# Batch 0's last gathers land beside each other and VectorE sums them, in a fused attention, expert and attention kernel

## Chip, cores and metric

The kernel runs on one core of a Trainium2 chip. The metric is the device time of one execution in microseconds (us), median of several runs. Every engine has its own instruction queue, taken in order: TensorE (PE), VectorE (DVE), ScalarE (ACT), GpSimd (POOL), and SyncE (SP), which issues plain DMAs. Gathers with a list of row numbers (indirect DMAs) are issued by GpSimd, and so are DMAs that add what they fetch onto their destination.

## The reference, cut to what matters

There are 8 batches of 256 tokens of 512 numbers: 2048 tokens. The second step, and the beginning of the third, are what this case is about.

```python
x = x + tanh(g_xattn[0]) * causal_attention(layernorm(x), ctx, ctx)
x = x + tanh(g_ffn[0])   * experts(layernorm(x))     # 32 experts, each token goes to 8 of them
x = x + tanh(g_xattn[1]) * cross_attention(layernorm(x), ctx, ...)
x = x + tanh(g_ffn[1])   * ternary_linear(layernorm(x))
# experts: every (token, choice) has a slot in an expert's table; y = silu(xg @ w_gate) * (xg @ w_up) @ w_down
#          out[token] += weight * y[slot]            for each of the token's 8 choices
# cross_attention: q = rms_norm(x @ w_q.T + b_q, g_q), k = rms_norm(ctx @ w_k.T + b_k, g_k), v = ctx @ w_v.T + b_v
#          softmax(q k.T / sqrt(32)) v for 16 heads, then @ w_o.T + b_o
```

## The kernel before

There are three stages, one block of instructions for each. A block ends in a barrier: no engine begins the next one before all have issued what they have in this one.

**layer0** is the first attention and sends each token's row to 8 slots of a table in DRAM. **experts** runs 160 tiles of 128 slots through the experts' weights. For a tile PE turns the rows (L1293), multiplies by gate and up (L1305), turns the hidden rows (L1316) and multiplies by down (L1329); ACT scales the result into `ysb` (L1379), and SP stores that to `y_tiles` in DRAM (L1162), counted on four semaphores `y_out`. GpSimd loads the raw weights of each expert to `raw` (two buffers), which DVE splits into halves `wh` and `wl`. **layer1** is the second attention and the ternary layer, a loop over the 8 batches with 16 attention steps each.

*The gathers.* A token's 8 results are fetched from `y_tiles` and added to its row of `xs` (the running x, all 2048 tokens in SBUF) at the beginning of layer1 and during it. One gather fetches 128 rows of 2 KB: one of the two token tiles `t` of a batch, one of 8 choices. "A turn" is the two gathers of one choice; each batch has 8 turns, 16 gathers. A gather that adds to the same rows as an earlier one waits until that has landed. The choices are sorted, so turn 0 of batch 0 needs only that all but the last 7 tiles are stored, turn 7 needs all of them (`add_first`).

In batch 0, even turns add into `xs` (semaphores `y_added`) and odd ones into a second buffer `odd` (`odd_added`); its first gather there is plain (L431), all others add (L430). Turns 0 to 3 are issued in the experts block, turns 4 to 7 in layer1's. Later batches have all 8 turns added into `xs` by `add_rows` (L430). Batch 1's 16 gathers follow at once, with small jobs of GpSimd between them: 4 gathers stand before its job "P1" and 4 before "P3", 8 behind. In every attention step `s` of batch `b` GpSimd does its jobs of the step, waits for step s's probabilities, and issues one gather for batch `b + 2`.

*The beginning of layer1.* Before batch 0's attention all engines run the lists `BEGIN1`. For one batch the work in pieces is:
- "sc", "T0", "T1": the context rows are split to fp16 halves by ACT (L1588) and DVE (L1653) and turned (PE L1548, ACT L1593). "P0", "P1": their product for K, 12 matmuls of 128x512 each (PE L1542), read out by DVE (L1659). PE needs the read of one product before it begins the next.
- "xc": layernorm's statistics of x by DVE (L1636, L1640, L1642, semaphore `x_var`), which need every gather of the batch; GpSimd makes the inverse root (L1615). "xn": DVE normalizes (L1646). "sx", "T2", "T3": the split and turn of that (ACT L1583, DVE L1653). "P2", "P3": the products for Q in batch 0, "P4", "P5" for V; in later batches P2 is V's and "P3", "P4" Q's.
- After a pair of products ACT squares and sums them (L1599), and GpSimd makes the factors of rms norm in three small operations (L1622, L1624, L1626). Its job "P1" is that for K; "P3" in batch 0 and "P4" in the others is that for Q. DVE's "r" (L1666) waits for the latter; "k0" to "k3" (L349, L355, L361) and "S0" to "S7" (L372, L379) make the heads' stacks from the results.

In the loop the pieces of the next batch are dealt out to steps by the table `PREP1`. For GpSimd it says "xc" at step 5, "P1" at step 7, "P4" at step 11; for DVE "xc" and "xn" at step 4 and "r" at step 10. An attention step on DVE begins with the row maxima for two steps ahead (L325), then ACT's exponentials (L293), PE's turn of the probabilities (L278) and the product with V (L258).

Of the kernel before, what the change touches and what calls it, by code (L numbers as in the profile page):

```python
# [18 lines left out]
P = 128  # L19
# [17 lines left out]
SENT = 6  # L37
LAST_ADDS = 4
BY_ACT = (1, 5)
# [70 lines left out]
def over_batches(first, body, last):  # L110
# [80 lines left out]
class Attention:  # L191
# [5 lines left out]

    def __init__(self, nc, sb, sem, bank, tag, causal, scale, v, id32, id16, idb, maskb):
# [9 lines left out]
        self.probs = sb(tag + "probs", [P, 2, 2, S])  # L208
        self.probsT = sb(tag + "probsT", [P, 2, 4 * P])
        self.sums = sb(tag + "sums", [P, 2, QT, NH])  # L210
        self.outT = sb(tag + "outT", [P, 2, QT, H])
# [171 lines left out]
class Shared:  # L383


    def __init__(self, nc, es):
# [26 lines left out]
        self.bank = [es.enter_context(nc.psum_tensor(f"bank{i}", [P, 512], F32)) for i in range(8)]  # L413
        room = sb("room", [P, 11 * H])
        self.vec = room[:, 0 : 7 * H].rearrange("p (k h) -> p k h", h=H)
        self.cbuf1 = room[:, 7 * H : 9 * H].rearrange("p (t h) -> p t h", h=H)
        self.odd = room[:, 9 * H : 11 * H].rearrange("p (t h) -> p t h", h=H)
        self.xe = room[:, 0 : 2 * QT * ROW].rearrange("p (a t r) -> p a t r", a=2, t=QT)
# [4 lines left out]
        self.y_out = [es.enter_context(nc.semaphore(f"y_out{i}")) for i in range(NY)]  # L423
        self.odd_added = [es.enter_context(nc.semaphore(f"odd_added{t}")) for t in range(QT)]

    def gather(self, nc, to, n, t, k, add):
# [6 lines left out]
    def add_first(self, nc, pool, turn, t):  # L433

        k, n = TOPK - 1 - turn, turn // 2
        if t == 0:
            for i in range(NY):
                pool.wait_ge(self.y_out[i], 16 * len(range(i, MT - k, NY)))
        if turn % 2:
            if n > 0:  # L440
                pool.wait_ge(self.odd_added[t], 16 * n)
            self.gather(nc, self.odd[:, t, :], 0, t, k, n > 0).then_inc(self.odd_added[t], 16)
        else:
            if n > 0:
                pool.wait_ge(self.y_added[t], 16 * n)
            self.gather(nc, self.xs[:, t, :], 0, t, k, True).then_inc(self.y_added[t], 16)

    def add_rows(self, nc, pool, n, i):

        turn, t = divmod(i, QT)  # L450
        done = TOPK * n + turn - TOPK // 2
        pool.wait_ge(self.y_added[t], 16 * done)
# [3 lines left out]
class Plan:  # L456


    def __init__(self, nc, es):
        def sb(name, shape, dt=F32):  # L460
# [21 lines left out]
        self.t_dve = sb("t_dve", [1, MT], I32)  # L482
        self.raw = sb("raw", [P, NR, WEXP])
        self.absum = sb("absum", [P, HC])
# [626 lines left out]
def experts(nc, shared, plan, proj, w_experts, mats, ternary, ctx, vecs):  # L1111

    es = ExitStack()
    with es:
# [81 lines left out]
        def _(pool):  # L1196
# [69 lines left out]
            for e in range(NR + 1, E):  # L1266
# [15 lines left out]
        def _(pe):  # L1282
# [120 lines left out]
        def _(dve):  # L1403
# [36 lines left out]
            for t in range(3):  # L1440
                e = dve.value_load(t_e[0:1, t : t + 1])
                if t == 0:
# [5 lines left out]
            def step(t):  # L1448
                code = dve.value_load(t_dve[0:1, t.column()])
                with dve.If((code & 1) > 0):  # L1450
# [8 lines left out]
def layer1(nc, shared, weights, ctx, out):  # L1459

    es = ExitStack()
    with es:
# [9 lines left out]
        vbuf = sb("vbuf", [P, 2, QT, H])  # L1472
        at = Attention(nc, sb, sem, bank, "l1_", False, D**-0.5 / (SC_Q * SC_K), vbuf, shared.id32, shared.id16, None, None)

# [19 lines left out]
        rsum = sb("rsum1", [P, QT, NH])  # L1494
        att = sb("att1", [P, QT, H])
        a16 = sb("a16", [P, QT, 2, H], F16)
# [3 lines left out]

        g_made, sc_made, both = sem("g_made"), sem("sc_made"), sem("both")
        y_added, ctx_in = shared.y_added, shared.ctx_in
# [127 lines left out]
        def dve_prep_(dve, b, piece, chain):  # L1630
            v = nc.vector
            k = int(piece[1]) if piece[1:].isdigit() else 0
            if piece == "xc":
                for t in range(QT):
                    dve.wait_ge(y_added[t], 16 * (TOPK * (b.n + 1) - TOPK // 2))
                    chain.mark(v.bn_stats(st6[:, 0, t, :], mine(b, t)))  # L1636
# [156 lines left out]
        def _(pool):  # L1793
# [13 lines left out]

            before = {"P1": 4, "xc": 0, "P3": 4}
            for piece in BEGIN1["pool"]:
# [4 lines left out]
            def body(b, prep, post):  # L1814
                for s in range(STEPS):
# [34 lines left out]
        def _(dve):  # L1850
# [65 lines left out]
def flamingo(nc, x, ctx, g_xattn, g_ffn, gate_w, w_experts, mats, vecs, ternary, out):  # L1916
    with ExitStack() as es:
        shared = Shared(nc, es)
        weights = Projections(nc, es)
        with ExitStack() as es_plan:  # L1920
            plan = Plan(nc, es_plan)
            layer0(nc, shared, plan, weights, x, ctx, g_xattn, g_ffn, gate_w, w_experts, mats, ternary)
# [39 lines left out]
```

## Time and profile before

| what | value |
|---|---|
| median of 3 runs | 1558.16 us (1550.44 to 1563.45) |
| span of the profiled execution, first to last instruction | 1525.3 us |
| median less the span | 32.9 us |
| busy share: PE, DVE, ACT, POOL | 86%, 64%, 60%, 34% |
| mean granted TensorE clock, share of 2.4 GHz | 0.939 |

The page gives no time of its own for the profiled execution, only its span; the runs' times hold some 33 us more, which lie ahead of and behind the instructions. Times of rows are us from the start of the span. In a timeline row stand the start, how long, engine, line, operation, what it writes and reads, and in brackets how long the engine was idle before it and what ended that. A row of a merged group has the time of all its instructions.

### The profile page before, as it was taken

How to read it: one execution, taken by the hardware profiler on the slowest of the kernel's cores; microseconds unless marked ns; L12 is line 12 of the kernel's file. 1: busy time of each engine (PE TensorE's matmuls, PEld its weight loads, DVE VectorE, ACT ScalarE, POOL GpSimd, SP SyncE). 2: the span in 40 equal slices, each digit the busy share in tenths (PEclk: the TensorE clock that was granted, in tenths of full speed). 3: DMA queues.
4: the chain of work that ended last, by engine and by line, in shares of the span. 5: the costliest groups of instructions: out<-in, count | busy, mean ns of one | idle time of the engine just before them, and what ended most of it. 6: DMA issues, size and time to landing. Idle time of an engine off the chain costs nothing.

```text
span 1525.3 us, 37150 instructions
## 1 busy us (share of the span) xinstructions
PE 1309.4 (86%) x10733; PEld 834.6 (55%) x10734; DVE 972.8 (64%) x2387; ACT 920.1 (60%) x2261; POOL 520.1 (34%) x531
## 2 busy tenths in 40 slices
PE   5888888837999999999999999477989889898984
PEld 3656655524556666665666666144556555555552
DVE  5888888755456665655655633255787777776853
ACT  4777777724556666666666666244766667667661
POOL 1044444455333433332000001665554444541000
PEclk9988888968999999999999999688999999999997
DMA  2044344458888767767676545775654555642000
GB/s 72 29 173 180 146 146 151 156 213 304 269 285 282 256 219 261 238 217 244 218 242 222 181 149 154 126 111 83 98 99 65 104 82 84 100 65 52 15 1 28
DMA packets 96131, 233.39 MB, mean 153 GB/s; under 512 B 11808, under 2 KB 11808, under 8 KB 91424
## 3 DMA queue, kind: packets, MB, share of 16 engines
q0 software_dynamic: 33712, 113.79, 29.8%
q1 hardware_dynamic: 62320, 118.34, 23.3%
q8 instruction: 55, 0.90, 0.3%
q14 instruction: 44, 0.36, 0.1%
HBM read 140.84 MB, written 91.24 MB: 152 GB/s over the span
## 4 chain that ended last, share of the span: by engine, by line
PE 45%; DMA 9%; DVE 9%; issue 8%; ACT 3%; POOL 3%; SPq 1%; DVEq 0%; ACTq 0%; POOLq 0%
PE bank L1305 18%; PE bank L1329 10%; PE bank L1542 6%; DMA xs<-y_tiles,slot_ix 5%; PE bank L1293 4%; PE bank L258 2%; PE bank L1316 1%; PE bank L278 1%; DMA xg<-x_slots 1%; DVE l_nmax L325 1%; PE bank L1548 1%; POOL xs L430 1%; DMA x_slots<-blank 1%; DVE l_stack L379 1%; PE bank L240 1%
## 5 line engine op out<-in xcount | busy, mean ns | idle before, releaser
L1305 PE MATMUL bank<-wh,xT 128*128 x1280 | 343.3, 330 | 4.7 <-DVE hp L1420 4.4
L430 POOL DMA_INDIRECT xs<-y_tiles,slot_ix x120 | 194.6, 1622 | 234.2 <-DMA y_tiles<-ysb 99.1
L293 ACT ACTIVATE l_probs<-bank,l_bias 128x256 f32<-128x256 f32 (+1 forms) x512 | 224.4, 449 | 64.4 <-DVE l_bias L327 64.0
L1305 PE MATMUL bank<-wl,xT 128*128 x640 | 211.4, 330 | 0.0
L325 DVE TENSOR_REDUCE l_nmax<-bank 128x2 f32<-128x512 f32 (+1 forms) x256 | 158.1, 617 | 70.8 <-PE bank L240 41.3
L1410 DVE SCALAR_TENSOR_TENSOR hv<-bank,sg 128x192 f32<-128x192 f32 x160 | 56.9, 356 | 227.5 <-ACT sg L1364 203.5
L1379 ACT ACTIVATE ysb<-bank,xg 128x512 f32<-128x512 f32 x160 | 109.9, 687 | 119.1 <-PE bank L1329 119.1
L305 ACT ACTIVATE l_probsT<-bank 128x512 f32<-128x512 f32 (+1 forms) x256 | 140.0, 547 | 65.6 <-PE bank L278 65.2
L1358 ACT ACTIVATE xT<-bank 128x1024 f16<-128x1024 f16 x160 | 162.5, 1016 | 15.0 <-PE bank L1293 14.8
L1305 PEld LDWEIGHTS bank<-wh,xT 128*128 128x128 f16 x1280 | 126.5, 99 | 81.3 <-issue 11.1
L1329 PE MATMUL bank<-wh,hT 128*128 x480 | 156.1, 380 | 0.9 <-issue 0.9
L240 PE MATMUL bank<-l_stack 128*128 128x256 f16 (+1 forms) x512 | 105.7, 275 | 59.1 <-ACT l_probs L293 49.3
L278 PE MATMUL bank<-id,l_probs 128*128 128x128 f32 x896 | 149.7, 286 | 2.1 <-ACT l_probsT L305 0.5
L699 POOL DMA_INDIRECT x_slots<-room,slot_ix x112 | 113.4, 1013 | 108.3 <-issue 47.0
L1542 PE MATMUL bank<-w_hi,halfT 128*128 128x512 f16 x384 | 125.9, 390 | 18.9 <-DVE accb L1659 17.1
L1200 POOL DMA_DIRECT2D raw<-in_experts_dram x30 | 16.8, 560 | 334.1 <-DVE wl L1436 333.8
L1364 ACT ACTIVATE sg<-bank 128x192 f32<-128x192 f32 x160 | 52.8, 330 | 113.8 <-PE bank L1305 113.8
L1329 PE MATMUL bank<-wl,hT 128*128 x320 | 121.4, 379 | 0.0
L1293 PEld LDWEIGHTS bank<-id,xg 128*128 128x128 f16 x1280 | 84.9, 99 | 58.7 <-DMA xg<-x_slots 22.6
L1293 PE MATMUL bank<-id,xg 128*128 128x128 f16 x1280 | 98.9, 221 | 19.1 <-DMA xg<-x_slots 18.9
L278 PEld LDWEIGHTS bank<-id,l_probs 128*128 128x128 f32 x896 | 102.6, 147 | 11.7 <-ACT l_probsT L305 7.4
L1436 DVE SCALAR_TENSOR_TENSOR wl<-raw,wh x64 | 95.4, 1491 | 20.0 <-issue 15.9
(246 smaller groups left out, 2538.1 us busy)
## 6 DMA issues: line engine op xcount, KB each, us to landing
xg<-x_slots SPq DMA_DIRECT2D x160, 272.0 KB, 2.8
y_tiles<-ysb SPq DMA_DIRECT2D x160, 256.0 KB, 2.5
raw<-in_experts_dram POOLq DMA_DIRECT2D x30, 1280.0 KB, 7.1
x_slots<-blank SPq DMA_DIRECT2D x33, 272.0 KB, 3.6
xs<-in_x_dram SPq DMA_DIRECT2D x8, 512.0 KB, 4.4
cbuf<-in_ctx_dram SPq DMA_DIRECT2D x8, 512.0 KB, 5.8
stage<-in_mats_dram POOLq DMA_DIRECT2D x4, 1024.0 KB, 7.8
room<-in_ctx_dram SPq DMA_DIRECT2D x8, 512.0 KB, 4.6
```

The source lines that it names most:

```text
L240: last = self.nc.tensor.matmul(o, self.stack[:, b.par, 0, h, qt * P : (qt + 1) * P], self.stack[:, b.par, 1, h, 0:nk], start=True, stop=no ...
L278: last = self.nc.tensor.transpose(self.pT[s % len(self.pT)][:, (2 * kt + u) * P : (2 * kt + u + 1) * P], self.probs[:, s % 2, u, kt * P : ...
L293: last = self.nc.scalar.activation(self.probs[:, s % 2, u, 0:nk], self.pS[s % 2][:, u * S : u * S + nk], ACT.Exp, bias=self.bias[:, s % 4, ...
L305: self.nc.scalar.activation(self.probsT[:, s % 2, 0:w], self.pT[s % len(self.pT)][:, 0:w], ACT.Copy).then_inc(self.probsT_made, 1)
L325: self.nc.vector.tensor_reduce(self.nmax[:, s % 4, :], v, AX, ALU.max).then_inc(self.max_made, 1)
L430: return nc.gpsimd.indirect_dma_start(to, None, self.y_tiles[0 : (MT + 1 - k) * P, :], ix, compute_op=ALU.add)
L699: nc.gpsimd.indirect_dma_start(shared.x_slots, bass.IndirectOffsetOnAxis(ap=slot_ix[:, QT * b.n + t, k % TOPK : k % TOPK + 1], axis=0), xe ...
L1293: last = nc.tensor.transpose(o[:, c * P : (c + 1) * P], rows[:, c * P : (c + 1) * P], id16[:])
L1305: last = nc.tensor.matmul(bGU[t.place % 2][:, 0:GU], xT[:, t.place % 2, xo + c * P : xo + (c + 1) * P], wp[:, bass.ds(w, 1), c * GU : (c + ...
L1329: last = nc.tensor.matmul(bY[t.place % 2][:, :], h, wp[:, bass.ds(w, 1), at : at + H].rearrange("p a w -> p (a w)"), start=k == 0, stop=k ...
L1358: nc.scalar.activation(xT[:, t.place % 2, :], bX[t.place % 2][:, :].bitcast(F16), ACT.Copy).then_inc(x_ready, 1)
L1542: last = nc.tensor.matmul(o, xT[:, xo + c * P : xo + (c + 1) * P], w[:, c * H : (c + 1) * H], start=n == 0, stop=n == len(todo) - 1)
```

## The change

Turns 4 to 7 of batch 0 become plain gathers, each to a place of its own; the places (`landed`, five of them, the first is the former `odd`) lie in the memory of the raw expert weights, which therefore becomes `late`, shared by all stages. Plain gathers wait for no other gather, only for the stores and, once, for the last weights' split. Turns 4 and 5 are now issued at the end of the experts block, turns 6 and 7 in layer1. Only turns 0 to 3 still add by DMA. DVE adds the five places to `xs` in pieces "g0" to "g4", ten additions instead of two, spread over the beginning of its list, and its "P0" now stands ahead of "g3", and "P1" ahead of "sx".

GpSimd's order changes: 3 gathers of batch 1 before "xc", 1 before "P1", 4 before "P3", 8 behind. In batch 0's steps it issues no gather at steps 0 to 5, two at each of steps 6 to 11, one at steps 12 to 15. Some buffers of layer1 (probabilities, their turned form, the attention's output, `att1`) move into `late`. Three loads of table values into registers get bounds.

```diff
-LAST_ADDS = 4
+FIRST_TURNS, ADDED_TURNS = 6, 4
...
-    dve=["sc", "xc", "xn", "P0", "sx", "P1", "P2", "k0", "k1", "P3", "S0", "S1", "S2", "S3", "r", "k2", "k3", "S4", "S5", "P4", "S6", "S7", "P5"])
+    dve=["g0", "g1", "sc", "g2", "P0", "g3", "g4", "xc", "xn", "P1", "sx", "P2", "k0", "k1", "P3", "S0", "S1", "S2", "S3", "r", "k2", "k3", "S4", "S5", "P4", "S6", "S7", "P5"])
...
-        if turn % 2:
+        if turn >= ADDED_TURNS:
+            self.gather(nc, self.landed[:, 1 + turn - ADDED_TURNS, t, :], 0, t, k, False).then_inc(self.rows_in[turn - ADDED_TURNS], 16)
+        elif turn % 2:
...
-            for turn in range(TOPK - LAST_ADDS):
+            pool.wait_ge(weights_ready, E)
+            for turn in range(FIRST_TURNS):
...
-                code = pe.value_load(t_pe[0:1, t.column()])
+                code = pe.value_load(t_pe[0:1, t.column()], min_val=0, max_val=E * E)
...
-            for turn in range(TOPK - LAST_ADDS, TOPK):
+            for turn in range(FIRST_TURNS, TOPK):
                 for t in range(QT):
                     shared.add_first(nc, pool, turn, t)
             added = [ROWS]
+            FIRST_ADDS = [0] * 6 + [2] * 6 + [1] * 4
...
-            before = {"P1": 4, "xc": 0, "P3": 4}
+            before = {"xc": 3, "P1": 1, "P3": 4}
...
                     if b.n + 2 < B:
                         pool.wait_ge(at.probs_made, STEPS * b.n + s + 1)
-                        add_next(1)
+                        add_next(1 if b.n else FIRST_ADDS[s])
...
             for piece in BEGIN1["dve"]:
+                if piece[0] == "g":
+                    i = int(piece[1])
+                    for t in range(QT):
+                        if i == 0:
+                            dve.wait_ge(y_added[t], 16 * ADDED_TURNS // 2)
+                            dve.wait_ge(shared.odd_added[t], 16 * ADDED_TURNS // 2)
+                        else:
+                            dve.wait_ge(shared.rows_in[i - 1], 16 * QT)
+                            dve.wait_ge(summed, QT * (i - 1) + t + 1)
+                        v.tensor_tensor(mine(b0, t), mine(b0, t), shared.landed[:, i, t, :], ALU.add).then_inc(summed, 1)
+                    continue
                 if piece == "xc":
-                    for t in range(QT):
-                        dve.wait_ge(y_added[t], 16 * TOPK // 2)
-                        dve.wait_ge(shared.odd_added[t], 16 * TOPK // 2)
-                        v.tensor_tensor(mine(b0, t), mine(b0, t), shared.odd[:, t, :], ALU.add).then_inc(both, 1)
-                    dve.wait_ge(both, QT)
+                    dve.wait_ge(summed, QT * (TOPK - ADDED_TURNS + 1))
```

## Rows read from the trace of the kernel before

**Rows 1.** Busy time by stretch: from:to, length, PE, PEld, DVE, ACT, POOL, clock, DMA share, GB/s.

```profile
400.00:940.00 540.00, 530.95 (x4031) 329.70 (x4030) 301.18 (x806) 332.76 (x576) 116.35 (x144) 0.99 0.69 230
962.00:990.00 28.00, 8.47 (x33) 3.88 (x34) 8.02 (x15) 6.13 (x9) 16.53 (x13) 0.61 0.68 113
```

**Rows 2.** The chain that ended last, 940 to 1100: start, us, what.

```profile
976.50 5.69 DMA room<-y_tiles,slot_ix
...
1019.42 4.98 DMA xs<-y_tiles,slot_ix
1024.40 0.26 issue
...
1043.78 0.77 POOL rstd L1615
```

**Rows 3.** Timeline of VectorE at the beginning of layer1.

```profile
964.32 1.29 DVE L1653 SCALAR_TENSOR_TENSOR l_parts<-room,l_parts 128x512 f16<-128x512 f32 x2 [8.93 <-ACT l_parts L1588]
...
982.29 0.69 DVE L1862 TENSOR_TENSOR xs<-xs,room 128x512 f32<-128x512 f32 x1 [1.28 <-DMA room<-y_tiles,slot_ix]
...
986.48 1.06 DVE L1646 TENSOR_SCALAR accb<-xs,mv,rstd 128x512 f32<-128x512 f32 x2 [0.85 <-POOL rstd L1615]
987.46 0.68 DVE L1659 SCALAR_TENSOR_TENSOR accb<-bank,room 128x512 f32<-128x512 f32 x1
```

**Rows 4.** Timeline of PE: first and second product's beginning, third's.

```profile
967.21 0.61 PE L1542 MATMUL bank<-w_hi,halfT 128*128 128x512 f16 x1 [0.26 <-ACT halfT L1593]
...
988.28 0.58 PE L1542 MATMUL bank<-w_hi,halfT 128*128 128x512 f16 x1 [16.21 <-DVE accb L1659]
...
995.29 0.39 PE L1542 MATMUL bank<-w_hi,halfT 128*128 128x512 f16 x1 [1.55 <-ACT halfT L1593]
```

**Rows 5.** Timeline of VectorE in batch 0's steps.

```profile
1035.57 0.69 DVE L1659 SCALAR_TENSOR_TENSOR accb<-bank,room 128x512 f32<-128x512 f32 x1 [1.01 <-PE bank L1542]
1044.57 1.05 DVE L1646 TENSOR_SCALAR accb<-xs,mv,rstd 128x512 f32<-128x512 f32 x2 [8.31 <-POOL rstd L1615]
...
1065.74 1.40 DVE L1666 SCALAR_TENSOR_TENSOR accb<-accb,rs,room 128x512 f32<-128x512 f32 x2
```

**Rows 6.** Timeline of GpSimd around the end of the experts block.

```profile
949.86 0.98 POOL L431 DMA_INDIRECT room<-y_tiles,slot_ix  x1 [0.30 <-issue]
...
959.80 1.53 POOL L430 DMA_INDIRECT room<-y_tiles,slot_ix  x1 [0.30 <-issue]
962.36 0.10 POOL L1794 MEMSET sc<- 128x2 f32 x1 [1.03 <-POOLq L1114]
...
963.30 1.54 POOL L430 DMA_INDIRECT xs<-y_tiles,slot_ix  x1 [0.80 <-POOL sc L1795]
```

**Rows 7.** DMAs, us to landing: all L430; one plain gather; the store issued at 958.3.

```profile
DMA to landing us min/median/max: 4.6/5.0/7.1
...
room<-y_tiles,slot_ix POOLq DMA_INDIRECT x1, 4.8
...
y_tiles<-ysb SPq DMA_DIRECT2D x1, 256.0 KB, 3.9
```

**Rows 8.** Timeline of ACT: Q's last square; step 6's exponentials.

```profile
1002.98 0.19 ACT L1599 ACTIVATION_READ_ACCUMULATOR junk<-accb 128x1 f32 x1
...
1046.71 0.45 ACT L293 ACTIVATE l_probs<-bank,l_bias 128x256 f32<-128x256 f32 x1
```

**Rows 9.** Timeline of GpSimd: job P3, batch 1's last gather, job P4.

```profile
1006.26 0.19 POOL L1622 TENSOR_SCALAR ss<-ss 128x2 f32<-128x2 f32 x1
...
1027.49 1.54 POOL L430 DMA_INDIRECT xs<-y_tiles,slot_ix  x1 [0.81 <-DMA xs<-y_tiles,slot_ix]
...
1064.26 0.19 POOL L1622 TENSOR_SCALAR ss<-ss 128x2 f32<-128x2 f32 x1 [1.93 <-ACT junk L1599]
```

**Rows 10.** Register instructions: SP's load with bounds; PE's load, one tile.

```profile
L1157 SPq SEQ_ASSERT  x160: 18/18/18, 342.3 to 939.4; - x160
...
L1335 PEldq TENSOR_LOAD <-t_pe x1: 303/303/303, 901.9 to 901.9; - x1
```

More of the change, by code:

```diff
@@ L191, with __init__ @@
 class Attention:
-    def __init__(self, nc, sb, sem, bank, tag, causal, scale, v, id32, id16, idb, maskb):
+    def __init__(self, nc, sb, sem, bank, tag, causal, scale, v, id32, id16, idb, maskb, held=None):
+        held = held or sb
         self.nc, self.causal, self.scale, self.v = nc, causal, scale, v
@@ L207, in __init__ @@
         self.bias = sb(tag + "bias", [P, 4, 2])
-        self.probs = sb(tag + "probs", [P, 2, 2, S])
-        self.probsT = sb(tag + "probsT", [P, 2, 4 * P])
+        self.probs = held(tag + "probs", [P, 2, 2, S])
+        self.probsT = held(tag + "probsT", [P, 2, 4 * P])
         self.sums = sb(tag + "sums", [P, 2, QT, NH])
-        self.outT = sb(tag + "outT", [P, 2, QT, H])
+        self.outT = held(tag + "outT", [P, 2, QT, H])
         self.hi_ready, self.parts_ready = sem(tag + "hi_ready"), sem(tag + "parts_ready")
@@ L413, in __init__ @@
         self.bank = [es.enter_context(nc.psum_tensor(f"bank{i}", [P, 512], F32)) for i in range(8)]
-        room = sb("room", [P, 11 * H])
+        room = sb("room", [P, max(9 * H, 2 * QT * ROW + 3 * QT * H)])
+        self.late = sb("late", [P, NR * WEXP])
         self.vec = room[:, 0 : 7 * H].rearrange("p (k h) -> p k h", h=H)
         self.cbuf1 = room[:, 7 * H : 9 * H].rearrange("p (t h) -> p t h", h=H)
-        self.odd = room[:, 9 * H : 11 * H].rearrange("p (t h) -> p t h", h=H)
+        LANDED = TOPK - ADDED_TURNS + 1
+        self.landed = self.late[:, 0 : LANDED * QT * H].rearrange("p (n t h) -> p n t h", n=LANDED, t=QT)
         self.xe = room[:, 0 : 2 * QT * ROW].rearrange("p (a t r) -> p a t r", a=2, t=QT)
@@ L424, in __init__ @@
         self.odd_added = [es.enter_context(nc.semaphore(f"odd_added{t}")) for t in range(QT)]
+        self.rows_in = [es.enter_context(nc.semaphore(f"rows_in{i}")) for i in range(TOPK - ADDED_TURNS)]
     def gather(self, nc, to, n, t, k, add):
@@ L438, in add_first @@
                 pool.wait_ge(self.y_out[i], 16 * len(range(i, MT - k, NY)))
-        if turn % 2:
+        if turn >= ADDED_TURNS:
+            self.gather(nc, self.landed[:, 1 + turn - ADDED_TURNS, t, :], 0, t, k, False).then_inc(self.rows_in[turn - ADDED_TURNS], 16)
+        elif turn % 2:
             if n > 0:
                 pool.wait_ge(self.odd_added[t], 16 * n)
-            self.gather(nc, self.odd[:, t, :], 0, t, k, n > 0).then_inc(self.odd_added[t], 16)
+            self.gather(nc, self.landed[:, 0, t, :], 0, t, k, n > 0).then_inc(self.odd_added[t], 16)
         else:
@@ L450, in add_rows @@
         turn, t = divmod(i, QT)
-        done = TOPK * n + turn - TOPK // 2
+        done = TOPK * (n - 1) + turn + ADDED_TURNS // 2
         pool.wait_ge(self.y_added[t], 16 * done)
@@ L456, with __init__ @@
 class Plan:
-    def __init__(self, nc, es):
+    def __init__(self, nc, es, shared):
+        self.raw = shared.late[:, :].rearrange("p (r w) -> p r w", r=NR)
         def sb(name, shape, dt=F32):
@@ L1440, in _ @@
             for t in range(3):
-                e = dve.value_load(t_e[0:1, t : t + 1])
+                e = dve.value_load(t_e[0:1, t : t + 1], min_val=0, max_val=E - 1)
                 if t == 0:
@@ L1448, in step @@
             def step(t):
-                code = dve.value_load(t_dve[0:1, t.column()])
+                code = dve.value_load(t_dve[0:1, t.column()], min_val=0, max_val=2**24)
                 with dve.If((code & 1) > 0):
@@ L1472, in layer1, with held @@
         vbuf = sb("vbuf", [P, 2, QT, H])
-        at = Attention(nc, sb, sem, bank, "l1_", False, D**-0.5 / (SC_Q * SC_K), vbuf, shared.id32, shared.id16, None, None)
+        LATER = dict(l1_probs=(0, 2 * 2 * S), l1_probsT=(2 * 2 * S, 2 * 4 * P), l1_outT=(8 * S, 2 * QT * H), att1=(8 * S + 4 * H, QT * H))
+        def held(name, shape, dt=F32):
+            first, n = LATER[name]
+            view = shared.late[:, first : first + n]
+            if dt == F16:
+                view = view.bitcast(F16)
+            letters = "abcd"[: len(shape) - 1]
+            sizes = {k: n for k, n in zip(letters, shape[1:])}
+            return view.rearrange(f"p ({' '.join(letters)}) -> p {' '.join(letters)}", **sizes)
+        at = Attention(nc, sb, sem, bank, "l1_", False, D**-0.5 / (SC_Q * SC_K), vbuf, shared.id32, shared.id16, None, None, held)
         w_hi, w_lo, vec = weights.w_hi, weights.w_lo, shared.vec
@@ L1494, in layer1 @@
         rsum = sb("rsum1", [P, QT, NH])
-        att = sb("att1", [P, QT, H])
+        att = held("att1", [P, QT, H])
         a16 = sb("a16", [P, QT, 2, H], F16)
@@ L1634, in dve_prep_ @@
                 for t in range(QT):
-                    dve.wait_ge(y_added[t], 16 * (TOPK * (b.n + 1) - TOPK // 2))
+                    if b.n > 0:
+                        dve.wait_ge(y_added[t], 16 * (TOPK * b.n + ADDED_TURNS // 2))
                     chain.mark(v.bn_stats(st6[:, 0, t, :], mine(b, t)))
```

5 lines of the change are left out of this document (2 added, 3 removed).

## The prediction

> **What bounds the kernel now.** I read the busy time by stretch first, then the chain of waits, then each engine's timeline where the chain leaves PE. In the experts stage PE is busy 530.95 of 540 us [rows 1]: nothing can be won there, only lost. From 962 to 990, the beginning of layer1, it is busy 8.47 of 28 us, at a mean clock of 0.61. The chain [rows 2] says why: it is on gathers, one behind the other, up to the last one of batch 0, issued at 976.50 and landed 5.69 us later. Then it follows GpSimd up to the inverse root of batch 1 at 1043.78. So the change works in the two places where the chain stands on gathers or on GpSimd's queue:
>
> Stall A, 972 to 988. VectorE is idle until the last gather lands, adds it at 982.29, and begins "xn" at 986.48, so 4.19 us later. The read of the first product stands behind that, at 987.46 [rows 3]; PE therefore waits 16.21 us with the second one [rows 4].
>
> Stall B, 1036 to 1045. VectorE waits 8.31 us for GpSimd's L1615 [rows 5], which stands in GpSimd's queue behind batch 1's gathers and five of batch 2's. Each gather on the same rows waits for the landing of the one two before it.
>
> **The end of the experts block.** GpSimd now issues turns 4 and 5 there. Its last gather before started at 959.80 and took 1.53 us, so it was free at 961.33, and layer1 began at 962.36 [rows 6]: GpSimd was nearly the last engine at the barrier. A plain gather occupies it for 0.98 us, and 0.30 go between two, 1.28 together, against 1.83 for one that adds [rows 6]. Four of them begin at 961.63; the store that turn 5 waits for was issued at 958.3 and landed after 3.9 us [rows 7], in time. GpSimd is free at 961.63 + 4 x 1.28 - 0.30 = 966.45, and layer1 begins at about 967.1 (the distance before was 1.03 us from the end of GpSimd, part of which was SP's last store; I take 0.65, bounds 0.4 and 1.1). Everything of layer1 that isn't waiting for gathers moves 4.7 us later. This is the price of the change.
>
> **Batch 0's landing.** Turns 6 and 7 begin 0.94 us after the block, as turn 4 did [rows 6], at 968.05, and the last of the four at 968.05 + 3 x 1.28, with 0.5 for the last store, about 972.1; it lands after 4.8 [rows 7], at 976.9, where the last landing before was 982.19 [rows 2]. Bounds: landings of 4.6 and of 7.1 [rows 7]. So the rows are there 5.3 us earlier, but VectorE can't use all of it: "P0" now stands before "g3". The first product began at 967.21, 4.85 us after the block, and lasted 4.9 at the half clock (PE was idle for 16.21 us before 988.28, so it ended at 972.07) [rows 4]; "g0" and "g1" ahead of "sc" add about 0.9, since the landing of turn 4 and two additions of 0.69 lie ahead of it. PE is done at 967.1 + 4.85 + 0.9 + 4.9 = 977.75. Then VectorE: 0.69 for the read, four additions of 0.71, 981.3. Before, the second addition ended at 982.98 [rows 3]. From there to "xn" it takes 3.5 us as before, and "xn" begins at 984.8. **Gain at "xn" 1.7 us**, bounds -1 and +4. The three gathers of batch 1 now ahead of GpSimd's inverse root cost nothing: the third waits for the first one's landing, 973.4 + 5.3 = 978.7, and is issued by 980.3, while the root isn't wanted before 984.
>
> **Behind "xn".** The second product is now done before it (its input, the context, was ready; it needs at most 4.9 us after 978.4). Before it held PE from 988.28 on, and T2 and T3 and ACT's copies waited for it, so that the third product began at 995.29 [rows 4]. Now T2 follows "sx" directly; ACT squares P0 and P1 first, and copies T2 at 989.5. The third product begins about 989.6. It probably runs at the half clock, because PE idles for 6 us before (the row of 988.28 shows 0.58 where that of 995.29 shows 0.39), which costs up to a third of 4.9 us. Q's last square ends at about 998.9, was 1003.17 [rows 8]: gain 4.3. GpSimd's job "P3" came only at 1006.26 [rows 9], 3.1 us behind the square, since it stood behind gathers 4 to 7. It stands behind four of them again. A gather lands in 5.0 us and 0.26 pass until the next on the same rows [rows 2, 7], so a pair is issued every 5.3 us: the four start at 990.0, 991.9, 995.3, 997.5, and "P3" at 999.1. "r" follows such a job by 1.5 us (1064.26 and 1065.74 for batch 1 [rows 5, 9]), so it stood at 1007.7; now it comes at 1000.8, behind it and VectorE's four stack copies: **gain 6.8 us** when the attention of batch 0 begins, bounds 3 and 9.
>
> **Stall B.** Batch 1's last gather was issued at 1027.49 [rows 9]. Now the last eight begin about 1000.5 and run in pairs of 5.3, with 2 us more where the context's load stands in the way (the 7.1 of [rows 7]): the last one at 1019 to 1021, landed by 1025.7, just when VectorE, 6.8 us earlier than before, asks. No gathers of batch 2 stand before the root any more. The next bound is VectorE's P1 read of batch 1, at 1035.57 [rows 5], now 1028.8. "xn" begins at 1029.5 instead of 1044.57: **gain 15.0 us** at this point.
>
> **Stall C, new.** The gathers left out in steps 0 to 5 have to be issued: two in each of steps 6 to 10 stand ahead of GpSimd's job "P4" at step 11, ten in all. They may start when the two exponentials of step 6 are done, 0.9 after 1046.71 [rows 8], 1047.6 before, now about 1032.6. They can't go faster than their landings: five pairs every 5.3 us, the last begins 21.2 us later and takes 3.4 us of GpSimd. "P4" begins at 1032.7 + 21.2 + 3.4 = 1057.3, and VectorE's "r" at 1058.8. Before, "P4" waited for ACT, not for gathers (the 1.93 us in brackets of its row), and began at 1064.26 [rows 9], "r" at 1065.74 [rows 5]. Moved 15 us forward, "r" would be wanted at 1050.7, so VectorE, and behind it the maxima of every step, waits 8.1 us. **Gain left: 6.9 us.** The bounds of the pair are 4.9 and 5.9 (the shortest landing of 4.6 [rows 7], and 5.69 as at 976.50 [rows 2]): "r" 1.6 us earlier, or 2.4 us later. Behind it GpSimd has the same number of gathers before it, relative to "r", as before, so I see nothing that gives or takes more; the later batches have the old order.
>
> **One answer.** Bounds on loads of registers add an assertion of 18 ns, if they do what they do on SP [rows 10]. PE's load of a tile takes 303 ns already, and the array is idle for only 9 of 540 us [rows 1], so such loads are hidden behind queued matmuls; if this one weren't, 160 x 18 ns = 3 us. The eight more additions on VectorE (5.5 us) lie in its idle time but for those counted. The moved buffers cost nothing: same sizes and engines.
>
> **The skill against the rows.** The rows say 4.6 to 7.1 us for a gather of 256 KB. The Trainium skill, page "DMA: Bandwidth & Descriptors", section "Anatomy of one DMA — SWDGE (gpsimd) path", gives about 2.0 us + bytes / 436e3 from start to end, 2.6 us here (an estimate from that page). By that rule GpSimd's issue would set the pace and rival (a) below would come true. The trace disagrees, with 4.6 at the least.
>
> **Rivals.** (a) Stall C is short, because GpSimd's own pace and not the landings sets the pair: 2 x 1.83 = 3.66 us [rows 6]. Then "P4" begins at 1032.7 + 14.6 + 3.4 = 1050.7 and "r" comes at 1052.2, 1.5 late only; the gain is 13.5, the time 1545. For it: landings come while GpSimd does other things, and in the old order "P4" never waited. Against it: each gather's wait for the one on the same rows is in the code, and the median landing is 5.0 [rows 7]. (b) The later barrier eats the rest: "g3" and "g4" stand behind a product at half clock, layer1 begins 1 us later than I count and the gain at "xn" is -1 instead of 1.7; batch 1's last gather lands late by as much; with stall C the sum is 0 to 4, 1556. For it: GpSimd was within 1 us of the barrier [rows 6]. Against it: the stores, the other bound there, are landed. (c) Slower, by the double gathers: stall C is longer than what A and B return. "r" is bound to step 6's exponentials: each microsecond by which they come later than 1032.6 goes to it undiminished, and from 1039.5 on nothing is left. If (b) holds (2.7 us) and all pairs take 5.9 because DMAs of the context and output share the engines (batch 1's last four: 2.4), they come at 1037.7, "P4" at 1037.8 + 23.6 + 3.4 = 1064.8, "r" at 1066.3, and PE, idle for 10 us and not 8, begins again at the half clock for 2 us more: 1561. For it: the 7.1 us landing [rows 7]; against it: the median.
>
> **Chances and range.** The sum is made against the profiled span, 1525.3 us; the median of the runs is 32.9 above it, and since nothing ahead of the span or behind it changes, the gain comes off the median. The likeliest, 6.9 us off: 1558.2 - 7 = **1551**, 45 in 100 (its own range 1546 to 1556). Rival (a) 20, (b) 22, (c) 13. The three runs lie 13 us apart, and a median may be 4 us off for that alone. The range takes in (a), (b) and most of (c): 1540 to 1563, with the runs' spread. What a measurement of this kernel can tell from no change is about 1%, 15.6 us: faster than 1542.6 only if (a) holds and the median falls low or VectorE's start gains its full bound, 11 in 100; slower than 1573.7 only if (c) holds at its worst, 3 in 100; within, 86.
>
> **What would show it.** In the changed profile: layer1 begins near 967; L1862 additions end near 981; a second product before "xn"; no wait of L1646 for L1615 beyond 1 us in batch 0's steps; but "r" (L1666) of batch 1 waits some 8 us for L1626, with PE and ACT idle beside it. Wrong if GpSimd isn't the last at the barrier, if gathers land in under 4 us, or if L1666 doesn't wait.

## The result and the profile after

| | median of the runs | profiled execution: time, span |
|---|---|---|
| before | 1556.26 us (1547.39 to 1563.45, 19 runs) | time not given, span 1525.3 |
| changed | 1562.76 us (1557.14 to 1570.24, 19 runs) | 1562.36, span 1560.6 |

The ratio is 1.0049 [1.0031, 1.0067]: the change costs about 7.6 us by the ratio, 6.5 by the medians, where a gain of 7 was forecast. The shown profiles of before and after must come from different chips, though no record says so. In the profile of before the first attention took 32 us less (its last row was sent at 329.21 instead of 360.88). All seven profiles taken later on two chips where before took 1521 to 1523 us show that row at 327 to 330, whichever kernel it was, and all five on two chips where before took 1555 to 1557 show it at 358 to 365. So spans are not compared here: positions are counted from the last tile's scaling, which is 960.84 before and 995.26 after, and times of kernels only by their ratio to the kernel before on the same chip. The profiled time of the changed kernel is 1.8 us above its span, so the 32.9 us that the prediction and the table of before put around the span were mostly the other chip.

The last tile of the kernel before, then of the changed one, in the timelines of ACT:

```profile
960.84 0.69 ACT L1379 ACTIVATE ysb<-bank,xg 128x512 f32<-128x512 f32 x1 [0.78 <-PE bank L1329]
```

```profile
995.26 0.69 ACT L1387 ACTIVATE ysb<-bank,xg 128x512 f32<-128x512 f32 x1 [1.29 <-PE bank L1337]
```

The changed kernel, timeline of GpSimd (compare [rows 6, 9]): last plain gather in the experts block, layer1's first instruction, the last of turns 6 and 7, job "P3", batch 1's last gather, root of batch 1, the first of the double gathers.

```profile
999.94 0.95 POOL L435 DMA_INDIRECT late<-y_tiles,slot_ix  x1 [0.30 <-DMA y_tiles<-ysb]
1000.89 0.11 POOL L1814 MEMSET sc<- 128x2 f32 x1
...
1005.07 0.95 POOL L435 DMA_INDIRECT late<-y_tiles,slot_ix  x1 [0.30 <-issue]
...
1031.59 0.19 POOL L1641 TENSOR_SCALAR ss<-ss 128x2 f32<-128x2 f32 x1
...
1053.75 1.55 POOL L434 DMA_INDIRECT xs<-y_tiles,slot_ix  x1 [1.58 <-DMA xs<-y_tiles,slot_ix]
1060.10 0.71 POOL L1634 TENSOR_TENSOR rstd<-mv,neghalf 128x2 f32<-128x2 f32 x1 [4.80 <-DVE mv L1662]
1065.40 1.59 POOL L434 DMA_INDIRECT xs<-y_tiles,slot_ix  x1 [4.58 <-ACT late L294]
```

The same kernel, timeline of VectorE (compare [rows 3, 5]; L1666 is "xn", L1686 is "r"):

```profile
1010.60 0.69 DVE L1679 SCALAR_TENSOR_TENSOR accb<-bank,room 128x512 f32<-128x512 f32 x1 [4.81 <-PE bank L1561]
1011.21 2.49 DVE L1888 TENSOR_TENSOR xs<-xs,late 128x512 f32<-128x512 f32 x4
...
1017.20 1.06 DVE L1666 TENSOR_SCALAR accb<-xs,mv,rstd 128x512 f32<-128x512 f32 x2 [0.85 <-POOL rstd L1634]
...
1032.89 1.42 DVE L1686 SCALAR_TENSOR_TENSOR accb<-accb,rs,room 128x512 f32<-128x512 f32 x2
...
1061.57 0.99 DVE L1666 TENSOR_SCALAR accb<-xs,mv,rstd 128x512 f32<-128x512 f32 x2
...
1093.74 1.42 DVE L1686 SCALAR_TENSOR_TENSOR accb<-accb,rs,room 128x512 f32<-128x512 f32 x2 [12.53 <-POOL rs L1645]
...
1120.21 0.17 DVE L1662 TENSOR_SCALAR mv<-mv 128x2 f32<-128x2 f32 x1
...
1126.52 1.00 DVE L1666 TENSOR_SCALAR accb<-xs,mv,rstd 128x512 f32<-128x512 f32 x2 [4.90 <-POOL rstd L1634]
```

Read down, it tells most of the story. The first "xn" and "r" come early, the wait of 8.31 us in [rows 5] is gone from the row at 1061.57, a new one of 12.53 us stands at 1093.74, and a larger one than before, of 4.90 instead of 1.87, at 1126.52. Counted from the last tile:

| point | before | after | gain | forecast |
|---|---|---|---|---|
| "xn" of batch 0 | 25.64 | 21.94 | 3.7 | 1.7 |
| "r" of batch 0 | 46.72 | 37.63 | 9.1 | 6.8 |
| "xn" of batch 1 | 83.73 | 66.31 | 17.4 | 15.0 |
| "r" of batch 1 | 104.90 | 98.48 | 6.4 | 6.9 |
| "xn" of batch 2 | 134.11 | 131.26 | 2.9 | 6.9 |
| end of the span | 564.46 | 565.34 | -0.9 | 6.9 |

The last line is known to a few us only: in the two later profiles with the layer1 of before (runs 1 and 8 below) the span ends 567.8 and 562.4 behind the last tile, in the two later ones with the changed one (runs 5 and 6) 563.2 and 564.8.

The chain that ended last, changed kernel, over the double gathers (start, us, what): every landing is a link up to the fifth pair, and the five starts are 5.96, 5.99, 5.68 and 5.88 us apart. The rows of 1065.40, 1071.36, 1077.35, 1083.03 and 1088.91 begin a pair; "issue" is time for which the profile shows no wait, here until GpSimd starts the next.

```profile
1065.40 5.20 DMA xs<-y_tiles,slot_ix
1070.65 0.71 issue
1071.36 5.16 DMA xs<-y_tiles,slot_ix
1076.56 0.79 issue
1077.35 4.86 DMA xs<-y_tiles,slot_ix
1082.25 0.78 issue
1083.03 5.06 DMA xs<-y_tiles,slot_ix
1088.13 0.78 issue
1088.91 1.54 POOL xs L434
1090.83 1.54 POOL xs L434
1092.72 0.73 POOL rs L1643
1093.74 0.76 DVE accb L1686
```

The second wait is in GpSimd's queue again. Its timeline in the changed kernel, at batch 1's first steps:

```profile
1118.40 1.55 POOL L434 DMA_INDIRECT xs<-y_tiles,slot_ix  x1 [1.13 <-ACT late L294]
1121.44 1.55 POOL L434 DMA_INDIRECT xs<-y_tiles,slot_ix  x1 [1.48 <-DMA xs<-y_tiles,slot_ix]
1124.17 1.55 POOL L434 DMA_INDIRECT xs<-y_tiles,slot_ix  x1 [1.18 <-DMA xs<-y_tiles,slot_ix]
1125.16 1.32 POOL L1634 TENSOR_TENSOR rstd<-mv,neghalf 128x2 f32<-128x2 f32 x1
```

Batch 2's statistics were done at 1120.38 (the row of 1120.21), but two gathers of batch 3, each waiting for a landing, still stood ahead of the root. Before, at the same place, only the last of them started after the statistics (1092.61 against 1091.80), and VectorE waited 1.87 us. The kernel before, timelines of VectorE (L1642 is the end of the statistics, L1646 "xn") and of GpSimd:

```profile
1091.63 0.17 DVE L1642 TENSOR_SCALAR mv<-mv 128x2 f32<-128x2 f32 x1
...
1094.95 1.00 DVE L1646 TENSOR_SCALAR accb<-xs,mv,rstd 128x512 f32<-128x512 f32 x2 [1.87 <-POOL rstd L1615]
```

```profile
1092.61 1.55 POOL L430 DMA_INDIRECT xs<-y_tiles,slot_ix  x1 [1.35 <-DMA xs<-y_tiles,slot_ix]
```

Within those few us, layer1 leaves the two kernels level. So the rest of the loss must lie elsewhere, and the trace has one more difference. Register instructions of PE's load of a tile's table entry, by line (minimum, median, maximum in ns), kernel before and then changed:

```profile
L1335 PEldq TENSOR_LOAD <-t_pe x160: 297/308/1375, 345.7 to 949.1; - x160
L1335 PEldq FUSED_REGOPS  x133: 42/42/42, 370.8 to 938.2; - x133
```

```profile
L1343 PEldq FUSED_REGOPS  x293: 42/151/165, 379.6 to 983.9; - x147
L1343 PEldq TENSOR_LOAD <-t_pe x160: 297/538/1566, 378.3 to 983.2; - x160
L1343 PEldq SEQ_ASSERT  x160: 18/18/28, 379.8 to 984.1; - x160
```

A bounded load is more than the assertion of 18 ns: 160 further register operations of about 151 ns come with it, and the load itself takes 538 ns in the median instead of 308. It takes 470 to 538 in all seven profiles of kernels with PE's bound and 307 to 314 in all seven without it. From the 29th tile to the last, the scaling went from 484.38 to 960.84 before, 476.5 us, and from 512.49 to 995.26 after, 482.8.

### The profile page after: what moved, and what is told of

Its sections match the earlier page's. It is cut to its first block and busy times, and to the rows that moved or that the text cites. A ratio compares the mean times of both kernels' runs of the same rounds, so it can differ in the third digit from the quotient of the medians.

```text
span 1560.6 us, 37807 instructions
## 1 busy us (share of the span) xinstructions
PE 1319.8 (85%) x10733; PEld 839.3 (54%) x10734; DVE 979.6 (63%) x2395; ACT 922.5 (59%) x2261; POOL 514.0 (33%) x531
## 5 line engine op out<-in xcount | busy, mean ns | idle before, releaser
L434 POOL DMA_INDIRECT xs<-y_tiles,slot_ix x116 | 186.5, 1608 | 237.9 <-DMA y_tiles<-ysb 99.1
L294 ACT ACTIVATE l_probs<-bank,l_bias 128x128 f32<-128x128 f32 (+1 forms) x256 | 105.6, 424 | 56.1 <-DVE l_bias L328 54.7
L294 ACT ACTIVATE late<-bank,l_bias 128x256 f32<-128x256 f32 x256 | 118.8, 474 | 15.8 <-DVE l_bias L328 14.7
L1207 POOL DMA_DIRECT2D late<-in_experts_dram x30 | 16.8, 560 | 337.0 <-DVE wl L1444 336.7
L1561 PE MATMUL bank<-w_hi,halfT 128*128 128x512 f16 x384 | 124.3, 385 | 3.4 <-DVE accb L1679 2.9
L306 ACT ACTIVATE late<-bank 128x512 f32<-128x512 f32 x128 | 76.7, 599 | 65.0 <-PE bank L279 65.0
L241 PEld LDWEIGHTS bank<-l_stack 128*128 128x128 f16 x512 | 46.3, 102 | 122.5 <-ACT l_probs L294 51.1
L1444 DVE SCALAR_TENSOR_TENSOR wl<-late,wh x64 | 95.4, 1492 | 26.2 <-issue 22.1
```

What stands on the lines that cost most here:

```text
L241: last = self.nc.tensor.matmul(o, self.stack[:, b.par, 0, h, qt * P : (qt + 1) * P], self.stack[:, b.par, 1, h, 0:nk], start=True, stop=no ...
L294: last = self.nc.scalar.activation(self.probs[:, s % 2, u, 0:nk], self.pS[s % 2][:, u * S : u * S + nk], ACT.Exp, bias=self.bias[:, s % 4, ...
L434: return nc.gpsimd.indirect_dma_start(to, None, self.y_tiles[0 : (MT + 1 - k) * P, :], ix, compute_op=ALU.add)
L1444: last = v.scalar_tensor_tensor(pick(wl, a, b), pick(raw, a, b), SC_W, pick(wh, a, b), ALU.mult, ALU.subtract)
L1561: last = nc.tensor.matmul(o, xT[:, xo + c * P : xo + (c + 1) * P], w[:, c * H : (c + 1) * H], start=n == 0, stop=n == len(todo) - 1)
```

## The experiments

Ratios are to the kernel before on the same chip. Microseconds worked out from a ratio are for a time of 1557 us throughout.

**Group 1: which part costs.** Runs 1 to 4 were taken on a chip where before takes 1520.6 us, runs 5 to 7 on one where it takes 1522.8. Run 1 is the kernel before with only the bounds:

```diff
-                code = pe.value_load(t_pe[0:1, t.column()])
+                code = pe.value_load(t_pe[0:1, t.column()], min_val=0, max_val=E * E)
...
-                e = dve.value_load(t_e[0:1, t : t + 1])
+                e = dve.value_load(t_e[0:1, t : t + 1], min_val=0, max_val=E - 1)
...
-                code = dve.value_load(t_dve[0:1, t.column()])
+                code = dve.value_load(t_dve[0:1, t.column()], min_val=0, max_val=2**24)
```

> The kernel before with nothing but the bounds on the register loads of PE and VectorE. It gives a profile of the old order that can be held beside the changed kernel's. Theory L (the changed kernel lost time outside layer1: its first attention lasts 30 us longer in its profile than in the one of before, yet the runs differ by 7): the long first attention is the usual state of both kernels and the profile of before was an unusual execution; then this span is about 1555 with the first gather near 973 to 979, and the time equals before within 3 us. Rival (the bounds cost): 160 loads times 18 to 60 ns on PE, 3 to 8 us slower than before, seen in the expert stage. Rival (code layout): any change of the instruction stream makes the first attention longer, time 5 us or more above before.

Measured: 1.0054 [1.003, 1.0079], 8.4 us slower. Its 29th to last tile took 482.7 us. So the bounds cost, a little more than that rival's 3 to 8 us; the first attention is as short as in the profile of before, so the theory and the rival of the code's layout fell.

Run 2, the changed kernel with the old pace of gathers in batch 0's steps:

```diff
-            FIRST_ADDS = [0] * 6 + [2] * 6 + [1] * 4
+            FIRST_ADDS = [1] * 16
```

> The changed kernel, but batch 0's steps issue one gather each, as before. Theory (stall C: ten gathers ahead of GpSimd's P4 cost 8 us, but without them stall B of 8 us returns): xn of batch 1 waits about 8 us for the inverse root L1634, r of batch 1 does not wait; the time is within 3 us of the changed kernel. Rival (the double gathers are the loss of the whole change): 6 to 8 us faster than the changed kernel, so equal to before or under it.

Measured: 1.0003 [0.9984, 1.0022]. The wait at batch 1's "xn" is back with 5.83 us, that at "r" is gone, and the gain over before at batch 2's "xn" is 9.4 us (134.11 against 124.68). The time is 5.9 us under run 5, the changed kernel, so the rival was right about the time, and the theory about the place of the waits.

Run 3, doubles moved behind "P4":

```diff
-            FIRST_ADDS = [0] * 6 + [2] * 6 + [1] * 4
+            FIRST_ADDS = [0] * 6 + [1] * 5 + [2] * 3 + [3, 2]
```

> The changed kernel, but the gathers that steps 0 to 5 leave out come behind P4: one in each of steps 6 to 10, two in steps 11 to 13, three in 14, two in 15. Theory (stall C): both stall B and stall C are gone, r of batch 1 does not wait, 8 us less there; the crowd of 11 gathers in steps 11 to 15 needs 11/2 times 5.3 = 29 us against some 20 of the steps, so batch 2's rows may be 5 us late and up to 5 come back there: 3 to 8 us faster than the changed kernel. Rival (the loss comes behind r in any case, since the sum of gathers is the bound): same as the changed kernel.

Measured: 1.0051 [1.0035, 1.0068]. "r" of batch 1 no longer waits (gain 18.1 there), and all but 0.6 us of it is lost at batch 2's "xn". The rival, that the loss comes behind "r" in any case, held. Its timeline of VectorE:

```profile
1086.08 0.69 DVE L1656 BATCH_NORM_STATS2 st<-xs 128x6 f32<-128x512 f32 x1 [8.07 <-DMA xs<-y_tiles,slot_ix]
...
1088.63 0.69 DVE L1656 BATCH_NORM_STATS2 st<-xs 128x6 f32<-128x512 f32 x1 [1.86 <-DMA xs<-y_tiles,slot_ix]
...
1100.33 1.00 DVE L1666 TENSOR_SCALAR accb<-xs,mv,rstd 128x512 f32<-128x512 f32 x2 [9.81 <-POOL rstd L1634]
```

Late rows first, then the root behind batch 3's gathers: 19.7 us of waits in place of the one of 12.5.

Run 4, turns 4 and 5 in layer1 again, plain as in the change:

```diff
-FIRST_TURNS, ADDED_TURNS = 6, 4
+FIRST_TURNS, ADDED_TURNS = 4, 4
```

> The changed kernel, but turns 4 and 5 are issued in layer1's block again, still plain and with places of their own. Theory (the barrier waits for GpSimd): layer1 begins 4 us earlier after the last tile, the first product ends 4 us earlier, the last landing comes at the same time or 0.5 us later, and xn 1 to 3 us earlier: 0 to 3 us faster than the changed kernel. Rival (the earlier issue is what gains): xn 3 us later, 3 us slower.

Measured: 1.0064 [1.0039, 1.0089]. Layer1 begins 1.52 us behind the last tile's scaling, as before the change, against 5.63 in the changed kernel, yet the first "xn" stands 22.52 us behind it, against 21.94. The 4 us by which the barrier is later are paid back by four gathers fewer behind it. Neither the theory nor the rival came true: the changed kernel's own first "xn" stands between 21.94 and 23.46 in two profiles, so the two are the same.

Run 5, the changed kernel again, and run 6, the same without PE's bound:

> The changed kernel itself, on the chip of these runs, to hold the others beside it. Theory S (sum of terms: gathers in places and VectorE's order gain 7 us in layer1, the steps' double gathers lose 8, the bounds or the new build lose 8): 7 to 9 us slower than before. Rival (the first attention, 30 us longer in its first profile, is part of the change): 30 us longer in the first attention here too.

Measured: 1.0041 [1.0028, 1.0055], 6.4 us, and the first attention is not longer on this chip, so the theory came near and the rival fell.

```diff
-                code = pe.value_load(t_pe[0:1, t.column()], min_val=0, max_val=E * E)
+                code = pe.value_load(t_pe[0:1, t.column()])
```

> The changed kernel without the bound on PE's load; VectorE's bounds stay. The trace of the first run shows 0.15 to 0.17 us of register work more per tile on PE. Theory (PE's bound is exposed in a part of the tiles): 4 to 8 us faster than the changed kernel, in the expert stage. Rival (VectorE's bounds, or chance of the build): same as the changed kernel within 2 us.

Measured: 1.0009 [0.9996, 1.0021]; 478.5 us from the 29th to the last tile. That is 5.0 us under run 5, as the theory said.

Run 7, the kernel before with the three bounds of run 1 and with GpSimd's new order, its places and additions left as they were:

```diff
-            before = {"P1": 4, "xc": 0, "P3": 4}
+            FIRST_ADDS = [0] * 6 + [2] * 6 + [1] * 4
+            before = {"xc": 3, "P1": 1, "P3": 4}
...
-                        add_next(1)
+                        add_next(1 if b.n else FIRST_ADDS[s])
```

> The kernel before with the bounds and the changed GpSimd order (3, 1, 4 gathers around the jobs; none at steps 0 to 5, two at 6 to 11), but batch 0's gathers added by DMA as before. Theory: batch 0's xn waits for GpSimd, since three gathers of batch 1 stand before its inverse root and the second and third wait for landings: 1 to 3 us lost there; stall B is gone (8 us), stall C costs 12 and more, batch 2's root 3 more; 6 to 10 us slower than the run with bounds only. Rival (the order alone is good and the places are bad): faster than that by 3 us or more.

Measured: 1.0088 [1.0056, 1.012], so 5.3 us more than with the bounds alone, a little under what was expected; "r" of batch 1 waits 12.85 us.

**Group 2: split the bounds, and mend.** Runs 8 to 11 were taken on a chip where before takes 1557.37 us, run 12 on one where it takes 1555.14. Run 8, the two bounds of VectorE in the kernel before:

> The kernel before with bounds on VectorE's two loads and none on PE's. All three bounds together cost 8.4 us (1.0054), and leaving PE's out of the changed kernel took 3.2 us off its ratio. If the prices add, 3 to 5 us slower than before are left (1.002 to 1.0033). If PE's bound alone is what costs (the array's sequencer is the one that can starve it), no difference. If VectorE's are the dear ones (it splits the weights, and the loads stand ahead of that), 5 to 8 us, 1.0035 to 1.005.

Measured: 1.0014 [0.9995, 1.0033]; 479.2 us from the 29th to the last tile. The interval rules out that VectorE's are the dear ones, not that they cost nothing.

Runs 9 to 11 are the changed kernel without PE's bound and with other paces in batch 0's steps. Run 9, the old pace:

```diff
-            FIRST_ADDS = [0] * 6 + [2] * 6 + [1] * 4
+            FIRST_ADDS = [1] * 16
```

> The changed kernel with one gather of batch 2 in each step of batch 0, as before, and without PE's bound: the places, VectorE's additions and GpSimd's order at the beginning stay. If the double gathers take back what the places give (about 8 us) and PE's bound costs 3, it is 8 to 11 us faster than the changed kernel: 0.996 to 0.998 of the time before. If instead the loss of the changed kernel is in its places or additions, it stays at 1.000 or above.

Measured: 0.9966 [0.9948, 0.9985]; "xn" of batch 1 stands 75.7 us behind the last tile, after a wait of 8.50, that of batch 2 125.7. The ratio is in the range expected.

Run 10:

```diff
+            FIRST_ADDS = [1] * 4 + [0] + [1] * 6 + [2] + [1] * 4
```

> As the run before it, but no gather of batch 2 at step 4, just ahead of GpSimd's root of batch 1, and two at step 11 instead. If the chain of landings is short of time everywhere, then what this gives at batch 1's normalization (one gather's 2.6 us off its wait of 5.8) is lost again by batch 2's normalization, and the time is that of the run before within 1 us. If the chain has slack between, 2 to 3 us faster than that run.

Measured: 0.9958 [0.9942, 0.9975], 73.0 and 125.0. The 2.7 us won at batch 1 have shrunk to 0.7 at batch 2, and the time is that of run 9 within the noise, as expected without slack.

Run 11:

```diff
+            FIRST_ADDS = [1] * 3 + [0] * 2 + [1] * 6 + [2] * 2 + [1] * 3
```

> As the same kernel with the old steps, but no gathers at steps 3 and 4 and two at each of steps 11 and 12. A whole pair is out of the way of batch 1's root: its wait of 5.8 us should nearly go. With slack in the chain 4 to 6 us faster than with the old steps; without slack equal to it, since batch 2's rows come a pair later (5.3 us) and its normalization waits for them.

Measured: 0.9951 [0.9929, 0.9973], 69.4 and 124.3; the 2.3 us to run 9 are within the noise. The wait at batch 1's "xn" fell to 0.16 us. At batch 2 most of it was given back, but not to late rows. This kernel's timelines of VectorE and of GpSimd:

```profile
1102.68 0.17 DVE L1662 TENSOR_SCALAR mv<-mv 128x2 f32<-128x2 f32 x1
...
1112.37 1.05 DVE L1666 TENSOR_SCALAR accb<-xs,mv,rstd 128x512 f32<-128x512 f32 x2 [8.23 <-POOL rstd L1634]
```

```profile
1104.19 1.55 POOL L434 DMA_INDIRECT xs<-y_tiles,slot_ix  x1 [1.53 <-DMA xs<-y_tiles,slot_ix]
1106.67 1.55 POOL L434 DMA_INDIRECT xs<-y_tiles,slot_ix  x1 [0.92 <-DMA xs<-y_tiles,slot_ix]
1110.02 1.55 POOL L434 DMA_INDIRECT xs<-y_tiles,slot_ix  x1 [1.80 <-DMA xs<-y_tiles,slot_ix]
1111.01 1.32 POOL L1634 TENSOR_TENSOR rstd<-mv,neghalf 128x2 f32<-128x2 f32 x1
```

The statistics are done at 1102.85; three gathers of batch 3 stand between them and the root. So in run 12 the same list was given to batch 1's steps:

```diff
-                        add_next(1 if b.n else FIRST_ADDS[s])
+                        add_next(FIRST_ADDS[s] if b.n < 2 else 1)
```

> As the kernel that skips steps 3 and 4, with the same list in batch 1's steps too (batch 3's gathers); all later batches as before. In the run before this one the statistics of batch 2 were done at 1102.85, but GpSimd's root came at 1111.01, behind two gathers of batch 3. If this queue is what holds batch 2's normalization (8.23 us of wait), then 4 to 6 us less: 0.992 to 0.993 of the time before, and the wait at xn of batch 2 falls to 1 to 4 us. If the landings of batch 2 are what holds it, the time stays at 0.995 and the wait stands at the statistics instead. A rival: batch 3's rows then come late, with a new wait at its normalization, where none is now.

Measured: 1543.77 us against 1555.14, **0.9923 [0.9901, 0.9945]**, faster than both kernels. By the ratios it is 6.7 us under run 9, and 4.4 under run 11, where the intervals overlap. "xn" of batch 2 stands 118.5 us behind the last tile, 5.7 earlier than in run 11, and waits 1.78 us, as expected. The rival, a new wait at batch 3, did not come: its "xn" stands at 180.2, was 186.0, and doesn't wait. Its timeline of VectorE, "xn" of batches 1 and 2:

```profile
1056.08 1.06 DVE L1666 TENSOR_SCALAR accb<-xs,mv,rstd 128x512 f32<-128x512 f32 x2 [2.74 <-POOL rstd L1634]
...
1105.54 1.00 DVE L1666 TENSOR_SCALAR accb<-xs,mv,rstd 128x512 f32<-128x512 f32 x2 [1.78 <-POOL rstd L1634]
```

## Why the prediction was wrong

The sum of parts, from the ratios at 1557 us: all three bounds +8.4 (1.0054); GpSimd's paused and doubled gathers +5.9 (1.0041 against 1.0003) or +6.7 (1.0009 against 0.9966, without PE's bound) in the changed kernel or, with GpSimd's order at the beginning, +5.3 (1.0088 against 1.0054) in the old one; places, additions, early turns and GpSimd's order at the beginning -7.9 (1.0003 against 1.0054) or -7.5 (0.9966 against 1.0014). The first values of the three add up to the +6.4 of run 5 by the way they are formed, and prove nothing; bounds and gathers in the old kernel (run 7, 1.0088) less the 7.5 make +6.2, where run 5 and the result have 6.4 and 7.6. This agreement is not built in. Each difference of two ratios has an interval of 3 to 6 us to either side (an estimate from the two intervals). Set against a kernel before that has the same bounds, the change is worth 0.8 us (1.0009 against 1.0014) to 2.0 us (1.0041 against 1.0054), where 6.9 were forecast.

**First failed step: "such loads are hidden behind queued matmuls; if this one weren't, 160 x 18 ns = 3 us".** Measured 8.4. I took the price from one row of another engine, the assertion of 18 ns [rows 10], and didn't ask what else comes with a bounded load. The rows above show the rest. PE's is the dear one: leaving it out took off 5.0 us (1.0041 to 1.0009) in the changed kernel, 5.8 (1.0003 to 0.9966) in the changed one with the old pace and 6.2 (1.0054 to 1.0014) in the old one, and VectorE's two are left with 2.2 us, an interval that includes zero. The tiles agree: from the 29th to the last the seven kernels with PE's bound took 480.6 to 483.1 us, the six experiments without it 478.4 to 479.8, the kernel before 476.5. That is 3 to 4 us for PE's; the other 2 I can't place, since the first 28 tiles vary by more (112 to 125 us) from profile to profile. That PE is starved of instructions because its sequencer is busier is what the rows suggest; it was not tried apart from the bound itself.

**Second failed step: "Behind it GpSimd has the same number of gathers before it, relative to "r", as before, so I see nothing that gives or takes more."** The number is not the same. The prediction has ten gathers of batch 2 ahead of "P4"; the old order, one in each of steps 0 to 10, has eleven. So one more is left for behind: between "P4" and batch 2's root stand eleven gathers in the changed kernel and ten in the one before. The wait of batch 2's "xn" for that root goes by this number in all 14 profiles:

| gathers between "P4" and batch 2's root | kernels | wait for the root, us |
|---|---|---|
| 10 | before, runs 1, 2, 8, 9, 12 | 1.16 to 2.44 |
| 11 | changed, runs 4, 5, 6, 7, 10 | 4.08 to 4.90 |
| 12 | run 11 | 8.23 |
| 16 | run 3 | 9.81, behind 9.9 for late rows |

Runs 9 to 12 differ in the gathers' pace alone. Stall B, which I had put down to the five gathers of the next batch ahead of the root, thereby came again one batch later. I had moved it, not removed it: a gather taken from ahead of one job of GpSimd stands ahead of the next. The gain of 6.4 us at "r" of batch 1 fell to 2.9 at the next "xn", 3.0 of it by the longer wait; what was left by the end is within the few us that profiles differ. Putting the doubles later (run 3) made it worse, 19.7 us; skipping just the two steps ahead of the root, in batches 0 and 1, left 2.7 and 1.8 us of the waits. What run 12 pushed on came to rest at batch 3: twelve gathers stand ahead of its root too, but from "r" to the next "xn" there are 36.2 us there, against 29.1 one batch earlier, and nothing waits.

**Stall C** was where it was forecast, with its size too small: 12.53 us instead of 8.1. Four pitches took 5.88 us each (1065.40 to 1088.91) and not 5.3: the landing of about 5.1, plus 0.7 to 0.8 until GpSimd starts the next, where I had counted the 0.26 of [rows 2]. That is 2.3 us. The first double came 0.6 us later behind "xn" than counted, and VectorE asked 1.5 us sooner (1081.21, 19.6 us behind "xn", where 21.2 were counted). The upper bound for the pair (5.9) was the right value. That the gain at "r", 6.4 us, is so near the forecast 6.9 is luck: "r" came 2.9 us later behind "xn" than counted, and "xn" 2.4 us earlier.

**The barrier** was right: layer1 began 4.1 us later (1000.89 is 5.6 us behind the last tile's scaling, 962.36 was 1.5), forecast 4.7. "This is the price of the change" was not: run 4 issues those four gathers behind the barrier and gains nothing.

**Batch 0's landing** gave 3.7 us instead of 1.7. The first product ran 4.4 us (1006.10 to 1010.51) and not 4.9 and started 4.5 us later than before and not 5.6; as forecast the product and not the landing set the time, with "g3" and "g4" behind its read. (The prediction's start of the last plain gather, 972.1, should be 972.4 by its own terms; nothing hangs on it.) **Behind "xn"** 5.4 us were gained, forecast 5.1, and up to the next "xn" 8.3 more, forecast 8.2.

**The rivals.** (a), the short stall C, fell: no pair came faster than 5.68 us (5.52 in run 6). The rule named in the prediction (the Trainium skill, page "DMA: Bandwidth & Descriptors", section "Anatomy of one DMA — SWDGE (gpsimd) path") would have made it true, and the trace disagrees once more, with landings of 4.86 to 5.20 us in the chain above against 2.6. (b) had the size of the layer1 part nearly right (0 to 4 us) with the wrong cause, since the barrier ate nothing. (c) had nearly the measured time (1561) and a part of the cause, the double gathers. It knew nothing of the bounds, so its time is in part luck, and it placed the loss at "r" of batch 1, which still gained 6.4 us.

## What to carry to other kernels

Price an instruction option by all the instructions it generates, on the engine that is the bound, and multiply by its trips; three harmless-looking bounds in loops of 160 cost 8.4 us, as much as the staging won (7.5 to 7.9). When a queue whose links are landings is paused to let a small job through, count the links that then stand between this job and the next, against before: each one more cost about 3 us of wait here. So skip only the links just ahead of the job, and do so at each job until a stretch comes that is long enough for the rest. A gain must be followed to the first later batch that no longer waits, not only to the next wait.

## What the runs showed of the hardware

- A bounded register load in PE's queue brings an operation of about 151 ns and an assertion of 18 ns beside the load (160 of each here), in VectorE's queue 190 and 23 ns. PE's load itself goes from 308 to 538 ns in the median, VectorE's stays at 307.
- An accumulating gather of 128 rows of 2 KB holds GpSimd for 1.55 us, a plain one for 0.95; two chains on different rows issue a pair every 5.7 to 6.0 us in the changed kernel, 5.5 to 6.6 in run 6.
- The same kernel takes 1521 to 1523 us on two chips and 1555 to 1557 on two others, and some 30 us of that lie in the first attention: two profiles must be lined up at an event, not at the start.
